# The order of the calls on four engines, from the fold of the queries to the fourth FFN turn, in a gated cross-attention block

## The reference

```
_xattn(q, mem):  scores = (q Wq' + bq)(mem Wk' + bk)' / 16
                 keep the 32 largest of the 154 scores of a row, softmax over them
                 return (attn (mem Wv' + bv)) Wo' + bo
x = x + tanh(g_xattn) * _xattn(layernorm(x), ctx)
h = relu(layernorm(x) W1 + b1)            # 256 -> 1024
x = x + tanh(g_ffn) * (h W2 + b2)         # 1024 -> 256
```

## Time and profile before

| | us |
|---|---|
| median of 3 runs | 273.31 (271.86 to 273.37) |
| the profiled execution, its own time | 269.96 |
| its span (first to last instruction) | 268.2 |
| PE busy in the span | 254.0 (95%), 1778 matmul instructions |
| DVE / ACT / POOL busy | 167.2 (62%) / 140.3 (52%) / 171.1 (64%) |
| granted TensorE clock | 1.000 of full speed |

### The profile page before, as it was taken

How to read it: one execution, slowest core, us unless ns; L and a number is a source line. 1 busy time by engine, 2 the same in 40 slices (tenths; PEclk the granted TensorE clock), 3 DMA queues, 4 the chain that set the end, 5 groups by cost and what they waited for, 6 DMA issues and landing times.

```text
span 268.2 us, 5316 instructions
## 1 busy us (share of the span) xinstructions
PE 254.0 (95%) x1778; PEld 232.6 (87%) x1778; DVE 167.2 (62%) x733; ACT 140.3 (52%) x305; POOL 171.1 (64%) x233
## 2 busy tenths in 40 slices
PE   7979997988989999999999999999999999999995
PEld 7856687988978998999899989999899988999994
DVE  1786868853979757964976578864786287412011
ACT  2486664565472556544456337452845266436551
POOL 3448778876793687478546856577555844784552
PEclk9999999999999999999999999999999999999999
DMA  6991005000150033002300060000200020002011
GB/s 216 410 414 37 0 1 189 16 2 0 38 199 0 4 99 136 4 0 92 147 0 2 6 229 4 0 0 3 79 0 4 0 78 2 0 4 79 0 42 39
DMA packets 7019, 17.26 MB, mean 64 GB/s; under 512 B 816, under 2 KB 2384, under 8 KB 6736
## 3 DMA queue, kind: packets, MB, share of 16 engines
q1 hardware_dynamic: 6720, 16.77, 17.3%
q10 hardware_dynamic: 272, 0.16, 0.2%
HBM read 12.44 MB, written 4.19 MB: 62 GB/s over the span
## 4 chain that ended last, share of the span: by engine, by line
PE 80%; DVE 6%; ACT 5%; POOL 3%; issue 3%; DMA 1%; POOLq 0%; SPq 0%; ACTq 0%; DVEq 0%
PE z_ps L396 11%; PE z_ps L398 10%; PE z_ps L397 10%; PE y_ps L413 10%; PE y_ps L409 10%; PE y_ps L408 10%; PE sc_ps L329 5%; PE pt_ps L348 2%; PE att_ps L364 2%; PE att_ps L367 1%; PE att_ps L365 1%; DMA wq_in<-w_q 1%; PE att_ps L366 1%; PE pt_ps L378 1%; PE att_ps L378 1%
## 5 line engine op out<-in xcount | busy, mean ns | idle before, releaser
L1173 POOL TENSOR_TENSOR hid_lo<-hid,hid_hi 128x256 fp32r<-128x256 f32 (+1 forms) x88 | 86.8, 989 | 62.0 <-ACT hid L710 61.2
L709 ACT ACTIVATE hid_hi<-z_ps,small_in 128x256 fp32r<-128x256 f32 (+1 forms) x88 | 50.2, 571 | 84.0 <-PE z_ps L398 82.9
L408 PE MATMUL y_ps<-w_hi,hid_hi 128*128 128x256 f32 x248 | 64.4, 288 | 0.0
L409 PE MATMUL y_ps<-w_lo,hid_hi 128*128 128x256 f32 x248 | 62.6, 281 | 0.0
L396 PE MATMUL z_ps<-x2nt_hi,w_hi 128*128 128x256 f32 (+1 forms) x176 | 61.0, 347 | 0.8 <-DVE x2nt_lo L934 0.5
L398 PE MATMUL z_ps<-x2nt_hi,w_lo 128*128 128x256 f32 (+1 forms) x176 | 58.4, 332 | 0.0
L397 PE MATMUL z_ps<-x2nt_lo,w_hi 128*128 128x256 f32 (+1 forms) x176 | 58.3, 331 | 0.0
L710 ACT ACTIVATE hid<-z_ps,small_in 128x256 f32<-128x256 f32 (+1 forms) x88 | 49.7, 565 | 0.0
L408 PEld LDWEIGHTS y_ps<-w_hi,hid_hi 128*128 128x128 f32 x248 | 46.7, 188 | 1.1
L409 PEld LDWEIGHTS y_ps<-w_lo,hid_hi 128*128 128x128 f32 x248 | 46.7, 188 | 1.0
L413 PE MATMUL y_ps<-w_hi,hid_lo 128*128 128x256 f32 x248 | 44.0, 282 | 0.4 <-POOL hid_lo L1173 0.4
(11 more groups left out here) (132 smaller groups left out, 403.9 us busy)
## 6 DMA issues: line engine op xcount, KB each, us to landing
x_ring<-x SPq DMA_DIRECT2D x8, 512.0 KB, 5.1
out<-x SPq DMA_DIRECT2D x15, 256.0 KB, 2.1
xt_in<-x_t SPq DMA_DIRECT2D x7, 512.0 KB, 3.7
w_in<-w SPq DMA_DIRECT2D x2, 1024.0 KB, 9.9
wvo_in<-w_vo SPq DMA_DIRECT2D x1, 513.0 KB, 7.0
xt_in<-x_t SPq DMA_DIRECT2D x2, 256.0 KB, 6.5
ctx_in<-ctx_t SPq DMA_DIRECT2D x1, 462.0 KB, 8.5
stacked<-values SPq DMA_DIRECT2D x9, 32.0 KB, 2.5
```

Of the source, the lines that this page charges most:

```text
L408: mm(ffn_sum(u, j), hid_hi[:, c % RING, rows], w2_hi[:, c, :], start=opens, stop=False, skip_group_check=True)
L409: mm(ffn_sum(u, j), hid_hi[:, c % RING, rows], w2_lo[:, c, :], start=False, stop=False, skip_group_check=True)
L709: func(hid_hi[:, c % RING, 0:width], z_ps[c % 2][:, 0:width], ACT.Relu, bias=b1[:, c:c + 1]).then_inc(hid_hi_made, 1)
L1173: nc.gpsimd.tensor_tensor(hid_lo[:, slot, 0:width], hid[:, slot, 0:width], hid_hi[:, slot, 0:width], ALU.subtract).then_inc(hid_lo_made, 1)
```

## The change

The calls are the same, with the same operands; their places in the four lists differ. Besides that, `wvo_in` is requested after the second half of `xt_in[0]`, the wait for `sbias_made` stands inside `scale_scores` (at groups 0 and 2) and not ahead of it, `topk(a, p, first, last)` is written as single `topk_round` calls, `first_values_to_lo` waits for its two copies one by one, and `other_rests_to_lo` gets its count of 18 as an argument. TensorE's list, whole up to the end of turn 1 and cut after it:

```diff
             bias_scores(0)
             scores(0, 0)
+            fold_values(0)
             scores(0, 1)
-            fold_values(0)
             fold_values(1)
             fold_value_bias()
             values_of(0)
             values_of(1)
+            transpose_picked(0, 0)
             make_keys(1, 0)
-            transpose_picked(0, 0)
             make_keys(1, 1)
             attend(0, 0)
-            scores(1, 0)
             bias_scores(1)
             values_of(2)
             values_of(3)
+            scores(1, 0)
             transpose_x2n(0, 0)
+            scores(1, 1)
             values_of(4)
-
             ffn_in(0, 0)
+            ffn_in(0, 1)
+            transpose_picked(0, 1)
             values_of(5)
-            ffn_in(0, 1)
             ffn_in(0, 2)
-            transpose_picked(0, 1)
+            ffn_in(0, 3)
             ffn_out(0, 0)
-            ffn_in(0, 3)
             attend(0, 1)
             ffn_out(0, 1)
             ffn_in(0, 4)
-            scores(1, 1)
+            scores(2, 0)
             ffn_out(0, 2)
             ffn_in(0, 5)
+            ffn_in(0, 6)
             ffn_out(0, 3)
-            ffn_in(0, 6)
+            ffn_in(0, 7)
             transpose_x2n(0, 1)
+            transpose_picked(1, 0)
             ffn_out(0, 4)
-            ffn_in(0, 7)
             ffn_out(0, 5)
-            transpose_picked(1, 0)
-
+            ffn_out(0, 6)
             ffn_in(1, 0)
-            ffn_out(0, 6)
             ffn_in(1, 1)
             ffn_out(0, 7)
             attend(1, 0)
             ffn_in(1, 2)
+            ffn_in(1, 3)
             ffn_out(1, 0)
-            ffn_in(1, 3)
+            ffn_in(1, 4)
             ffn_out(1, 1)
-            ffn_in(1, 4)
-            scores(2, 0)
+            ffn_in(1, 5)
             ffn_out(1, 2)
-            ffn_in(1, 5)
+            ffn_in(1, 6)
+            transpose_x2n(1, 0)
             ffn_out(1, 3)
-            transpose_x2n(1, 0)
-            ffn_in(1, 6)
+            ffn_in(1, 7)
             ffn_out(1, 4)
-            ffn_in(1, 7)
+            ffn_in(2, 0)
+            scores(2, 1)
+            transpose_picked(1, 1)
             ffn_out(1, 5)
...
+            ffn_in(3, 0)
+            ffn_out(2, 6)
+            attend(2, 0)
+            ffn_out(2, 7)
+            ffn_in(3, 1)
...
+            ffn_in(3, 6)
+            scores(3, 1)
+            transpose_x2n(2, 0)
+            ffn_in(3, 7)
+            ffn_out(3, 4)
+            transpose_x2n(2, 1)
+            ffn_out(3, 5)
+            ffn_out(3, 6)
+            ffn_out(3, 7)
```

ScalarE, up to the first turn, and the place of `copy_values(5)`:

```diff
             take_tanh()
             widen_bv()
+            exps(0, 0)
             fold_wvo()
+            w1_to_hi(0)
             scale_bv()
-            exps(0, 0)
-            w1_to_hi(0)
+            copy_values(0)
+            copy_rest(0, 0)
+            pt_to_hi(0, 0)
+            copy_values(1)
+            exps(0, 1)
+            copy_keys(1, 0)
+            copy_keys(1, 1)
             w1_to_hi(1)
-            copy_values(0)
-            copy_values(1)
-            copy_rest(0, 0)
-            copy_keys(1, 0)
-            pt_to_hi(0, 0)
-            exps(0, 1)
-            copy_keys(1, 1)
             w2_to_hi(0)
...
             relu(0, 0)
-            copy_values(5)
...
             relu(0, 6)
+            copy_values(5)
             x2nt_to_hi(0, 1)
```

VectorE, the first group and the end of the list:

```diff
             pick(0, 0)
             scale_scores(0, 1)
-            topk(0, 1, 0, 1)
             pt_to_lo(0, 0)
-            topk(0, 1, 1, 2)
+            topk_round(0, 1, 0)
+            topk_round(0, 1, 1)
             residual(0, 0)
...
             topk_round(3, 0, 1)
+            x2nt_to_lo(2, 0)
             x2nt_to_lo(2, 1)
+            output(1, 0)
+            topk_round(3, 0, 2)
```

GpSimd:

```diff
             prepare()
             rstd_x(0, 0)
-            rstd_x(0, 1)
             stack_first_rest()
             scale_bo()
+            scale_b2()
             add_value_bias()
+            place_other_rests()
+            rstd_x(0, 1)
+            first_values_to_lo()
             w1_to_lo(0)
-            first_values_to_lo()
+            normalise_x2(0, 0)
             w1_to_lo(1)
-            place_other_rests()
-            scale_b2()
-            normalise_x2(0, 0)
             rstd_x(1)
             w2_to_lo(0)
...
             hid_to_lo(0, 4)
+            normalise_x2(0, 1)
             w2_to_lo(3)
-            normalise_x2(0, 1)
...
             hid_to_lo(1, 1)
+            add_b2(0, 0)
+            hid_to_lo(1, 2)
+            normalise_x2(1, 0)
+            hid_to_lo(1, 3)
+            hid_to_lo(1, 4)
             add_b2(0, 1)
-            hid_to_lo(1, 2)
-            hid_to_lo(1, 3)
-            other_values_to_lo()
-            hid_to_lo(1, 4)
-            normalise_x2(1, 0)
             hid_to_lo(1, 5)
-            add_b2(1, 0)
             hid_to_lo(1, 6)
             hid_to_lo(1, 7)
+            other_values_to_lo()
+            rstd_x(3)
...
             hid_to_lo(3, 7)
+            add_b2(1, 1)
+            add_b2(2, 0)
+            add_b2(2, 1)
             rstd_x(4)
```

More of the change, by code:

```diff
@@ L498, in _ @@
             ffn_in(1, 2)
+            ffn_in(1, 3)
             ffn_out(1, 0)
-            ffn_in(1, 3)
+            ffn_in(1, 4)
             ffn_out(1, 1)
-            ffn_in(1, 4)
-            scores(2, 0)
+            ffn_in(1, 5)
             ffn_out(1, 2)
-            ffn_in(1, 5)
+            ffn_in(1, 6)
+            transpose_x2n(1, 0)
             ffn_out(1, 3)
-            transpose_x2n(1, 0)
-            ffn_in(1, 6)
+            ffn_in(1, 7)
             ffn_out(1, 4)
-            ffn_in(1, 7)
+            ffn_in(2, 0)
+            scores(2, 1)
+            transpose_picked(1, 1)
             ffn_out(1, 5)
-            transpose_picked(1, 1)
-            ffn_in(2, 0)
             ffn_out(1, 6)
             ffn_in(2, 1)
+            ffn_in(2, 2)
+            attend(1, 1)
             ffn_out(1, 7)
-            attend(1, 1)
-            ffn_in(2, 2)
+            ffn_in(2, 3)
             ffn_out(2, 0)
-            scores(2, 1)
-            ffn_in(2, 3)
+            scores(3, 0)
+            ffn_in(2, 4)
             ffn_out(2, 1)
-            ffn_in(2, 4)
+            ffn_in(2, 5)
             ffn_out(2, 2)
-            ffn_in(2, 5)
-            ffn_out(2, 3)
             transpose_picked(2, 0)
             transpose_x2n(1, 1)
+            ffn_out(2, 3)
             ffn_in(2, 6)
+            ffn_in(2, 7)
             ffn_out(2, 4)
-            ffn_in(2, 7)
-            attend(2, 0)
             ffn_out(2, 5)
-            scores(3, 0)
             ffn_in(3, 0)
             ffn_out(2, 6)
+            attend(2, 0)
+            ffn_out(2, 7)
             ffn_in(3, 1)
-            ffn_out(2, 7)
+            ffn_out(3, 0)
+            ffn_in(3, 2)
+            ffn_in(3, 3)
             transpose_picked(2, 1)
[L542 to L545, removed]
+            ffn_out(3, 1)
+            ffn_out(3, 2)
+            ffn_in(3, 4)
             attend(2, 1)
-            ffn_out(3, 1)
-            ffn_in(3, 4)
-            ffn_out(3, 2)
             ffn_in(3, 5)
@@ L749, in _ @@
             relu(0, 5)
+            copy_rest(1, 0)
             relu(0, 6)
-            copy_rest(1, 0)
+            copy_values(5)
             x2nt_to_hi(0, 1)
@@ L754, in _ @@
             pt_to_hi(1, 0)
+            exps(1, 1)
             relu(1, 0)
@@ L758, in _ @@
             relu(1, 2)
-            exps(1, 1)
             relu(1, 3)
+            relu(1, 4)
             other_rests_to_hi()
-            relu(1, 4)
             relu(1, 5)
             x2nt_to_hi(1, 0)
+            copy_rest(1, 1)
             relu(1, 6)
-            copy_rest(1, 1)
             relu(1, 7)
+            exps(2, 0)
+            relu(2, 0)
             pt_to_hi(1, 1)
-            relu(2, 0)
-            exps(2, 0)
             relu(2, 1)
@@ L774, in _ @@
             relu(2, 3)
+            copy_rest(2, 0)
             relu(2, 4)
-            copy_rest(2, 0)
             relu(2, 5)
@@ L780, in _ @@
             relu(2, 6)
+            relu(2, 7)
             exps(2, 1)
-            relu(2, 7)
+            copy_rest(2, 1)
             relu(3, 0)
-            copy_rest(2, 1)
             relu(3, 1)
+            relu(3, 2)
             pt_to_hi(2, 1)
-            relu(3, 2)
             relu(3, 3)
-            x2nt_to_hi(2, 0)
             relu(3, 4)
             relu(3, 5)
-            exps(3, 0)
             relu(3, 6)
+            x2nt_to_hi(2, 0)
             relu(3, 7)
             x2nt_to_hi(2, 1)
+            exps(3, 0)
             for g in range(2, GROUPS - 1):
@@ L871, in scale_scores @@
                     dve.wait_ge(norm1_step, 2 * (a + 2))
+                if p == 0 and a % PER_BATCH == 0 and a <= PER_BATCH:
+                    dve.wait_ge(sbias_made, a // PER_BATCH + 1)
                 rstd = norm1[a % 2][:, 1, :]
@@ L984, in _ @@
+            topk_round(1, 1, 0)
             stats_x(2)
-            scale_scores(1, 1)
             x2nt_to_lo(0, 1)
-            topk(1, 1, 0, 1)
```

(25 more changed lines are left out.)

55 lines of the change are left out of this document (28 added, 27 removed).

## The result

The changed kernel takes 259.26 us in the median of 4 runs (258.68 to 259.71), the kernel before 272.59 in 4 (269.68 to 273.37): a ratio of 0.953, interval 0.945 to 0.961. The two profiled executions are 269.96 and 258.68 us, spans (first to last instruction) 268.2 and 256.8.

A forecast was written before the change was run, and what follows sets the result against it. Up to turn 4, PE's work plus order-made waits (8.84 us) bound the kernel. Gains 1.7 + 2.3 + 4.2 = 8.2, less 0.5, gave 7.7: 273.3 - 7.7 = 265.6 us for the median, range 263.0 to 269.0.

The forecast's parts named there:

- 8.84 is also the most that order can give.: Keys to turn 4: PE's 8.84 us without a matmul taken as the upper limit of the gain.
- 18.41 us as the work of turn 0: ffn_in(0, 0) to attend(1, 0): PE's measured busy time, same-sized matmuls in both orders, taken as 18.41 us plus waits.
- The replay and the sum: New lists replayed, turn 4 starting at 91.3 plus tight places; gains 1.7 + 2.3 + 4.2 = 8.2 us.
- a `w1` landing at 27 us: Slower rival, ahead of turn 0: w1 landing after 15.05 delays ACT, DVE and PE one for one; at 27, 276; chance 4%.
- A difference I leave as it is.: Whole kernel: the runs' median, 273.31, lies 3.35 us above the profiled 269.96; carried unchanged into the forecast.
- Half a microsecond allowed for tight places: Places with under 0.5 us of margin: some slip, 0.5 together, bounds nothing to 1.7, leaving gain 7.7.
- Ahead of turn 0: Keys to ffn_in(0, 0): of 2.30 us idle, 0.15 stays and a new wait of 0.45 comes; gain 1.7.
- Turns: Turn 0 and turns 1 to 3: PE's waits for x2n and those behind them go, gains 2.3 and 4.2 us.
- the 1.17 and 0.48 come from the 2.36: Turns 1 to 3: late x2nt_to_lo(1, 0) held back DVE's rounds for (2, 0), causing the later waits of 1.17 and 0.48.
- Hand-off and DMA edits: Turn 4 on: late pick(3, 0) and hid_lo(4, 0) covered by double-width ffn_in, no cost; wvo_in lands about 10.7, needed at 11.5.
- The rule weighed: Shared SBUF port: whether POOL also waits for DVE's two-input operations; if so, gain about 7 us; chance 10%.
- the 1.2 us of the rival: POOL's full stretch between 27 and 46.6 us pushed by 1.2 if POOL waits for DVE's picks; chance 10%.

The follow-up runs named there:

- x2n_late: Changed kernel with GpSimd's other_values_to_lo put back ahead of normalise_x2(1, 0), making x2n late: median 260.42 us.
- before_look: Kernel before, no edit, one profiled execution to see where a long one spends its time: 273.17 us.
- copy_first: Kernel before with ScalarE's copy_values(0) moved ahead of w1_to_hi(0): median 269.64 us, ratio 0.993.
- one_call: Kernel before with GpSimd's other_values_to_lo moved from ahead of hid_to_lo(1, 4) to behind hid_to_lo(1, 7): median 268.52 us.
- new_prelude: New lists and new order of the first two DMAs up to ffn_in(0, 0), the kernel before's lists from there: median 270.66 us.
- new_turns: Old lists and DMA order up to ffn_in(0, 0), scores(1, 1) put at their end, the changed kernel's lists from there: median 262.66 us.
- after_again: Changed kernel once more, no edit: median 258.77 us.
- old_dma_order: Changed kernel with wvo_in requested ahead of the second half of xt_in[0], as in the kernel before: median 258.80 us.
- gap_back: Changed kernel with ScalarE's w1_to_hi(1) moved up directly behind w1_to_hi(0), lengthening the prelude's wait: median 259.67 us.

## Why the prediction was wrong
The order of events was right nearly call by call; two costs of an idle TensorE were missing from the sum. Worked from the two medians, the 13.3 us are: 8.5 of idle time (8.8 to 0.36) for a forecast 7.7; 2.4 of busy time in the same matmuls (82.90 to 80.49 between keys and turn 4), forecast at nothing; 0.5 at both ends of the span, mostly the start of the keys (8.62 to 8.27), less 0.1 outside the span; and 2.0 because the kernel before's median lies 2.6 above its profiled execution and the changed kernel's 0.6. The forecast was 6.3 us too high, 265.6 for 259.26: 0.8 by the idle time, 2.4 by the busy time, 0.4 by the ends, and 2.8 by the 3.35 that it carried along where 0.6 were left.

- **"8.84 is also the most that order can give."** This step failed: keys to turn 4 became 10.87 us shorter. It takes a profile's idle time for the whole cost of a wait. Around one wait it is 0.2 us more in the rows of x2n_late, 0.3 over its stretch, and 0.26 to 0.30 a wait over the kernels with seven to ten; for the nine waits of the kernel before that makes the 2.4. The use of 18.41 us as the work of turn 0 failed with it, since those 18.41 held three waits.
- **The replay and the sum.** The replay put turn 4 at 91.3, which is 82.7 us after the keys (measured 80.85) and 9.0 ahead of 100.34. That is more than the 8.2 of the sum, and more than the 8.84 called the most; the prediction went by the sum and did not ask where the difference came from. One smaller slip: by its own rule, a `w1` landing at 27 us gives 277, and 276 belongs to 26 us.
- **"A difference I leave as it is."** This step failed too. I carried the 3.35 us between the median and the profiled execution into the forecast. Nearly all of it was the low clock behind two of the waits, and it went with them. before_look shows the two stretches, 1.6 and 1.5 us; by the mean clocks, 52 of 63 executions had at least one; copy_first, where the wait of 1.60 is split, had no run with both. That the later one goes with its wait is argued from one_call (1.3 us for 2.36, no run of six with both) and from the changed kernel's clock of 1.000, not tried by itself. Had I taken the 3.35 for that, the forecast would have been 262.3 for the profiled execution, and as much for the median: still 3 us too high, by the first step.
- **Half a microsecond allowed for tight places.** None slipped. `x2n(0, 0)`, `w1_to_lo(1)`, `pt_lo(2, 1)` and `x2n(2, 1)`, with margins of 0.15 to 0.45, all came in time.
- **Ahead of turn 0.** Right: one new wait, forecast 0.45, measured 0.36; `rstd_x(0, 1)` late and harmless (DVE stood still 1.28 for it); `w1_to_lo(1)` done at 28.93 (26.57 + 2.36), just ahead of the first `ffn_in` at 29.04. But the gain of 1.7 is no sum of its own. new_prelude alone gives 1.2, as the wait for `x2n(0, 1)` grows by 1.0.
- **Turns.** Right in that they carry most. Wrong in one reason: I had the 1.17 and 0.48 come from the 2.36. one_call took 1.05 off the first and left the others, and x2n_late brought the first back in part, without them. What removed them is somewhere in the new order of the turns (new_turns has none of them); which engine's list or which call was not tried one by one.
- **Hand-off and DMA edits.** Right: turn 4 to the end is as long as before, the swap of the transfers does nothing.
- **The rule weighed.** VectorE's second operation of `pick(0, 0)` took 0.83 us, where most take 0.31, and ended 0.17 behind `add_value_bias` on GpSimd. That one had started while the first operation ran, and took 0.83 for its 0.73 in the earlier trace rows:

```profile
16.06 0.31 DVE L896 SCALAR_TENSOR_TENSOR picked<-left,probs 128x154 f32<-128x154 f32 x1
16.29 0.83 DVE L896 SCALAR_TENSOR_TENSOR picked<-left,probs 128x154 f32<-128x154 f32 x1
```

```profile
16.12 0.83 POOL L1090 TENSOR_TENSOR vo_bias<-vo_part 128x256 f32<-128x256 f32 x1 [3.22 <-ACT vo_part L653]
```

It is the same in all five profiles in which VectorE's first operation started 0.06 to 0.07 us ahead of `add_value_bias` (the changed kernel, after_again, old_dma_order, new_prelude, x2n_late); in the eight in which `add_value_bias` started first it took 0.73, and in gap_back, where the two do not meet, 0.72. So GpSimd is held too, by 0.1 us here, but `hid_to_lo` kept its mean of 739 ns in the turns, and nothing near the 1.2 us of the rival was added. The Trainium skill (SBUF — State Buffer, "Who interferes with whom") lets whoever starts first hold the port pair; the rows agree with both directions of it.

## What to carry to other kernels
On the engine that bounds a kernel, a wait can cost more than its idle time in the profile: here 0.2 to 0.3 us more each, and nothing more in the one case in the middle of an accumulation. If the time of a kernel comes in clusters, look at the mean clock of each run first: a median that lies above the profiled execution can be a cost that only some executions show, and that the right change removes. And an engine that is put ahead by one edit waits longer at the next place where another engine's chain is due, so edits of an order are worth what they give together.

## What the runs showed of the hardware
The granted clock halved, from 2.4 to 1.2 GHz, behind the wait of 1.60 us in three of five profiles and behind the one of 2.3 to 2.4 in one of five; it stayed at full speed behind waits of 1.64, 1.19 and 1.15, and in new_prelude's profile behind one of 2.68. PE had been busy up to both waits of before_look (1.87 of the 2 us from 16 us on, 2.00 of those from 59 on). Each low stretch cost 1.5 to 1.6 us. I had not expected it, as the one profile of the kernel before showed 1.000 throughout. And PE's busy time in the same matmuls grew by 0.26 to 0.30 us with each wait, beside its idle time.
